# Moving the list of clipped edges and the search for leftovers from the window attention to the normalisation and the graph router's loop

## What is computed

```python
h = tok(x)                                   # patches times W
h = h + window_attention(layernorm(h))       # windows of 64 nodes, 8 heads
h = h + graph_moe(layernorm(h))              # router by attention over 262144 edges, 4 experts
h = h + image_attention(layernorm(h))        # batch norm behind it
h = h + moe(layernorm(h))                    # 8 experts, two chosen
```

```python
h = (x_flat @ W_gat).reshape(M, HEADS, NUM_EXPERTS)
e = leaky_relu(a_src[src] + a_dst[dst]);  ee = exp(e - e_max[dst])
denom = segment_sum(ee, dst);  msg = h[src] * (ee / denom[dst])
agg = segment_sum(msg, dst) + b_gat
```

## Time and profile before

| | |
|---|---|
| three runs | 872.81 us median (872.68 to 873.22) |
| the profiled execution | 871.04 us, span 869.2 us |
| busy in the span | PE 575.1, DVE 579.1, ACT 267.6, POOL 319.0 us |
| window attention | about 70 to 320 us |
| normalisation ln1 | about 320 to 348 us |
| router ahead of its loop | about 348 to 386 us |
| router's loop | about 386 to 572 us |
| mean granted TensorE clock | 0.673 of 2.4 GHz |

### The profile page before, as it was taken

The page is one execution under the profiler, slowest core; times in us unless marked ns, Lnnn a source line. Parts: engine busy times, 40 slices in busy tenths (PEclk is TensorE's granted clock), DMA queues, the critical chain, the costliest instruction groups (busy, mean ns, idle before and its releaser), DMA issues. The chain is left out here.

```text
span 869.2 us, 12176 instructions
## 1 busy us (share of the span) xinstructions
PE 575.1 (66%) x4215; PEld 346.1 (40%) x4215; DVE 579.1 (67%) x1309; ACT 267.6 (31%) x485; POOL 319.0 (37%) x373
## 2 busy tenths in 40 slices
PE   5517669756788859306766377624957772798886
PEld 4414446434466538203322233214935541522222
DVE  6985999999996472389876496566342438555453
ACT  1124223212222333013333042321043434545453
POOL 6013223122333402477777777700021110234334
PEclk9996655556688855556655565555557985589898
DMA  6100000000000000501111112000000000000001
GB/s 181 28 1 1 1 2 1 0 1 1 1 2 2 1 2 0 79 10 35 36 35 21 22 35 36 8 0 1 1 0 1 2 1 0 1 1 0 13 14 24
DMA packets 28633, 13.05 MB, mean 15 GB/s; under 512 B 22080, under 2 KB 25761, under 8 KB 28322
## 3 DMA queue, kind: packets, MB, share of 16 engines
q1 hardware_dynamic: 23842, 10.82, 5.2%
q0 software_dynamic: 4736, 1.51, 2.1%
HBM read 10.77 MB, written 1.54 MB: 14 GB/s over the span
## 5 line engine op out<-in xcount | busy, mean ns | idle before, releaser
L1453 POOL DMA_INDIRECT edge_scratch<-src_rows_dram,slot_src_index x144 | 156.7, 1088 | 46.7 <-issue 43.1
L599 POOL TENSOR_TENSOR wa_scores<-wa_scores,wa_max 128x512 f32<-128x512 f32 x32 | 37.1, 1160 | 163.5 <-DVE wa_max L780 163.5
L490 POOL TENSOR_TENSOR ln_xs<-xn,ln_stats 128x256 f32<-128x256 f32 x32 | 19.4, 615 | 154.8 <-DVE ln_stats L458 93.2
L644 PE MATMUL wa_s_ps<-wa_kbd,wa_qk 64*64 64x512 f32 x128 | 55.7, 960 | 29.8 <-issue 29.7
L543 PE MATMUL ln_pT<-ident,ln_xs 128*64 128x128 f32 (+1 forms) x112 | 28.0, 413 | 49.4 <-POOL ln_xs L490 48.7
L2054 POOL TENSOR_TENSOR moe_acc<-moe_acc,moe_weighted 128x512 f32<-128x512 f32 x28 | 37.7, 1347 | 49.7 <-DVE moe_weighted L1995 49.6
L1995 DVE SCALAR_TENSOR_TENSOR moe_weighted<-moe_y_ps,moe_b_cols,moe_G 128x512 f32<-128x512 f32 x32 | 24.0, 750 | 47.3 <-ACT moe_G L1968 43.9
L1574 PE MATMUL moe_h_ps<-xT,moe_w 65*128 65x512 f32 x64 | 54.1, 994 | 0.0
L737 ACT ACTIVATE wa_probsT<-wa_t_ps 128x512 f32<-128x512 f32 x32 | 19.1, 597 | 105.4 <-PE wa_t_ps L652 105.4
L1954 ACT ACTIVATE moe_hidden<-moe_h_ps,moe_b_cols 128x1024 f32<-128x1024 f32 x32 | 35.5, 1113 | 41.3 <-PE moe_h_ps L1886 41.3
L1894 PE MATMUL moe_y_ps<-moe_hidden,moe_w 128*64 128x512 f32 x128 | 39.0, 689 | 4.4 <-ACT moe_hidden L1954 2.3
(11 more groups left out here) (390 smaller groups left out, 1378.4 us busy)
## 6 DMA issues: line engine op xcount, KB each, us to landing
edge_onehot_T<-slot_lo_dram SPq DMA_DIRECT2D x16, 288.0 KB, 3.3
edge_scratch<-src_rows_dram,slot_src_index POOLq DMA_INDIRECT x144, 2.4
edge_scratch<-in_L_ffn_edge_index SPq DMA_DIRECT2D x2, 1024.0 KB, 6.3
xrow<-in_x SPq DMA_DIRECT2D x4, 256.0 KB, 7.8
out_h<-h SPq DMA_DIRECT2D x4, 256.0 KB, 2.6
moe_w<-in_L_ffn_W SPq DMA_DIRECT2D x3, 256.0 KB
src_rows_dram<-src_rows SPq DMA_DIRECT2D x1, 320.0 KB
moe_w<-in_L_ffn_W SPq DMA_DIRECT2D x2, 128.0 KB
```

Of the source, the lines that this page charges most:

```text
L599: pool.tensor_tensor(sc[b][:], sc[b][:], bc(mx[b][:], WIN), ALU.subtract).then_inc(shifted, 1)
L644: ins = pe.matmul(s_ps[b][half], qk[b][half, 0, :], kbd[b][half])
L1453: pool.indirect_dma_start(gs[b][:, j, :], None, srow_dram, bass.IndirectOffsetOnAxis(edges.src_index[:, x:x + 1], axis=0))\
```

## The change

The computation is the same; the order, two buffers and one engine differ.

- `PREFIX_STEP` goes from 9 to 7 and `MOVE_STEP` from 15 to 12; `take_last` is gone from the waiting loops.
- The rest of the generator waits for `now = TILES`, which only `ln1` sets. `ln1` pulls the digits of the first 512 columns and seven passes. The router's chunks pull two pieces each: four passes over 512 columns and seven over 1024, the two counts of leftovers, the digits of the last 160 columns.
- The counts of a chunk follow a table: 2, 1, 1, 1, 1, 1, 2, 3, 0, 1, 3, 3, 3, 2, 2, 2.
- `find_more` moves from ahead of the loop into chunk `REDUCE` = 8, GpSimd's reduction behind the gathers of chunk 8; the loop over the leftovers moves to chunk 9 (GpSimd: after the gathers of chunk 10).
- ScalarE does `save`, behind its GELUs.
- The router's buffers `xspread`, `hs`, `val`, `left` and `parts` move out of the memory that the leftovers lie in, into `list_onehots`.

```diff
-PREFIX_STEP, MOVE_STEP, MOVES, RING = 9, 15, 2, 6
+PREFIX_STEP, MOVE_STEP, MOVES, RING = 7, 12, 2, 6
...
-        while self.now < PREFIX_STEP + 2:
-            take_last()
+        while self.now < PREFIX_STEP + 1:
             yield
...
             while self.now <= MOVE_STEP + (j - RING) // MOVES:
-                take_last()
                 yield
...
         while self.now < TURN_STEP:
-            take_last()
             yield
...
-        while took < len(takes):
-            take_last()
+        while self.now < TILES:
             yield
-        self.after(dve, dve.memset(self.last_found[:, 512 + 8 * took:LC], 0.0))
+        self.split(dve, slice(0, 512), self.digits)
+        yield
+        took = 512
+        for start, width, passes in LAST_TAKES:
+            for _ in range(passes):
+                self.largest(dve, self.last_found[:, took:took + 8], rest[:, EC + start:EC + start + width])
+                took += 8
+                yield
+        self.after(dve, dve.memset(self.last_found[:, took:LC], 0.0))
...
-        node, digit = self.digits
-        self.after(dve, dve.tensor_scalar(node, self.last_found[:], 1.0 / M, -1.0, ALU.mult, ALU.add))
+        self.split(dve, slice(512, LC), self.late_digits)
+        yield
+
+    def split(self, dve, part, digits):
+
+
+        node, digit = (x[:, 0:part.stop - part.start] for x in digits)
+        self.after(dve, dve.tensor_scalar(node, self.last_found[:, part], 1.0 / M, -1.0, ALU.mult, ALU.add))
         self.after(dve, dve.tensor_scalar(digit, node, 6, None, ALU.arith_shift_right))
...
-    room = edges.rest[:, GX * TILES * NV:]
+    room = edges.room[:].bitcast(F32)[:, 2 * SIDE * P:]
...
-    MIDDLE = RCHUNKS // 2
+    REDUCE, MIDDLE = RCHUNKS // 2, RCHUNKS // 2 + 1
+    ends = list(itertools.accumulate((2, 1, 1, 1, 1, 1, 2, 3, 0, 1, 3, 3, 3, 2, 2, 2)))
+    assert ends[-1] == COUNT_CHUNKS
+    counts_of = [range(a, b) for a, b in zip([0] + ends, ends)]
...
-            for _ in lists:
-                pass
             match(0)
             match(1)
             spread(0)
-            edges.find_more(dve)
-            trips = dve.value_load(edges.limits[0:1, 1:2], min_val=1, max_val=XC // GX)
...
-                for u in (2 * c, 2 * c + 1):
-                    if u < COUNT_CHUNKS:
-                        count(u)
-                if c > 0:
-                    save(c - 1)
+                for _ in range(2):
+                    next(lists, None)
+                for u in counts_of[c]:
+                    count(u)
+                if c == REDUCE:
+                    edges.find_more(dve)
+                    trips = dve.value_load(edges.limits[0:1, 1:2], min_val=1, max_val=XC // GX)
...
-            gather(0)
-            edges.reduce_counts(pool)
-            for c in range(1, RCHUNKS):
+            for c in range(RCHUNKS):
                 gather(c)
+                if c == REDUCE:
+                    edges.reduce_counts(pool)
...
+            def save(c):
+
+                act.wait_ge(y_done, c + 1)
+                act.activation(ys[c % 2][c // 8][:, c // 2 % 4 * 512:(c // 2 % 4 + 1) * 512], y_ps[c % 2][:],
+                               ACT.Identity, bias=k.b2_0[:, c % 2:c % 2 + 1]).then_inc(y_saved, 1)
...
                 for u in (2 * c, 2 * c + 1):
                     gelu(u)
+                if c > 0:
+                    save(c - 1)
...
+            def pull(dve, c):
+                edges.now = TILES
+                next(lists, None)
+
             norm("ln0")
             with stage() as m:
                 window_attention(nc, m, k, xT, h, edges, lists)
-            norm("ln1", weight=k.wgat[:], out=hg, beside=lambda dve, c: next(lists, None))
+            norm("ln1", weight=k.wgat[:], out=hg, beside=pull)
```

More of the change, by code:

```diff
@@ L17 @@
+import itertools
 import math
@@ L836, in __init__ @@
         self.digits = [self.scratch[:, x * LC:x * LC + LC].bitcast(I32) for x in range(2)]
+        self.late_digits = [self.room[:].bitcast(F32)[:, 8192 + x * RC:8192 + x * RC + RC].bitcast(I32) for x in range(2)]
         self.last_lo, self.last_hi = mem.sb("last_dst_lo", [P, LC], BF16), mem.sb("last_dst_hi", [P, LC], BF16)
@@ L988, in form @@
         assert self.now < PREFIX_STEP, self.now
-        takes = [(start, width) for start, width, passes in LAST_TAKES for _ in range(passes)]
-        took = 0
-        def take_last():
-            nonlocal took
-            if took < len(takes):
-                start, width = takes[took]
-                x = 512 + 8 * took
-                self.largest(dve, self.last_found[:, x:x + 8], rest[:, EC + start:EC + start + width])
-                took += 1
-        while self.now < PREFIX_STEP + 2:
-            take_last()
+        while self.now < PREFIX_STEP + 1:
             yield
@@ L1232, in graph_router @@
     xohi = room[:, GX * P:GX * (P + TILES)].rearrange("p (c q) -> p c q", c=GX)
-    xspread = edges.rest[:, 0:GX * TILES * NV].rearrange("p (c t v) -> p c t v", c=GX, t=TILES)
     iota16 = loop.sb("iota_bf16", [P, P], BF16)
@@ L1369, in more @@
                 dve.wait_ge(more_used, i + 1)
-            def save(c):
-                dve.wait_ge(y_done, c + 1)
-                dve.tensor_scalar(ys[c % 2][c // 8][:, c // 2 % 4 * 512:(c // 2 % 4 + 1) * 512], y_ps[c % 2][:],
-                                  k.b2_0[:, c % 2:c % 2 + 1], None, ALU.add).then_inc(y_saved, 1)
             dve.memset(nobody[:, 0:W], 0.0).then_inc(nobody_ready, 1)
@@ L1442, in _ @@
             take(RCHUNKS - 1)
-            save(RCHUNKS - 1)
+            for _ in lists:
+                raise AssertionError
         @block.gpsimd
@@ L1529, in _ @@
                         act.activation(xval[:, :, :, GE], xe[:, 0], ACT.Exp).then_inc(more_exp, 1)
+            save(RCHUNKS - 1)
         @block.tensor
```

13 lines of the change are left out of this document (6 added, 7 removed).

## The result

| | before | after |
|---|---|---|
| median of four runs | 872.74 us (868.62 to 873.22) | **847.65 us** (844.64 to 852.13) |
| ratio | | 0.9746, 95% interval 0.9702 to 0.9791 |
| the profiled execution | 871.04 us, span 869.2 | 844.70 us, span 842.9 |
| mean granted TensorE clock | 0.673 | 0.706 |

The forecast was 866.9 us, range 856 to 873. The direction was right, the time 19 us too high and outside the range.

A forecast was written before the change was run, and what follows sets the result against it. The attention was taken as bound by VectorE, the router's loop by GpSimd's gathers; -13.1 + 1.5 + 3.5 - 1.4 + 3.6 = -5.9 from 871.04 gives 865.1, and 1.77 for the median makes 866.9 us, range 856 to 873.

The forecast's parts named there:

- Up to turn 22 VectorE never stands still, and the turns are as long as their edge work.: Attention: VectorE is the bound; a pass removed from turns 6 to 22 saves its length, down to an empty step's.
- Turns 6 and 7 become empty, clock at 0.50: 2 x 6.36.: Attention: these two turns, without edge work, take 6.36 us each with TensorE at 1.2 GHz, together 12.7 us.
- Turns 25 to 29 are five empty ones. I take 6.36: 31.8.: Attention: five turns without edge work take 6.36 us each, TensorE at the lower clock, together 31.8 us.
- Rival 1: Attention, turns 6, 7 and from 25: TensorE granted 2.4 GHz; total 855, or 858.4 with the last five alone; chance 0.20.
- The prelude at nothing: Router ahead of its loop: removing 17.7 us of VectorE work gains nothing, since VectorE then waits for chunk 0's rows.
- The wait at the leftovers, +3.5: Router's loop: GpSimd, having issued chunks 9 and 10, waits for the leftovers' keys from VectorE, costing 3.5 us.
- The end of the loop, +3.6: Router, chunk 15: two counts now stand before the last output, costing 3.6 us.
- rival 2: Router's loop: VectorE comes late to chunk 8, each microsecond lengthening GpSimd's wait by one; 5 give 872; chance 0.12.
- I take 0.7: Router's loop: each count beside the gathers costs GpSimd 0.7 us, so two counts moved into chunk 15 give -1.4.
- Rival 4: Router's loop: the new pieces hold up gathers as the one-hots do, costing 12 us; total 879; chance 0.08.
- The last stage at nothing: From the save of the first logits to the end, code the change doesn't touch: forecast difference 0.
- Rival 3: Attention, turns 10 to 12: the moves' matmuls come on top of a step, losing some 6 us; 873; chance 0.10.

The follow-up runs named there:

- the second chip: The changed kernel, unaltered, run again in five rounds on another chip: median 853.1 us against 868.1 for the kernel before, ratio 0.9807.

## Why the prediction was wrong, step by step

- **"Up to turn 22 VectorE never stands still, and the turns are as long as their edge work."** Right for the terms built on it: turns 8 to 19 took 100.77 (forecast 100.8), 20 to 22 took 13.97 (14.0). A pass taken out of turns 6 to 10 was worth far less than its length (26.5 us of passes gave 3.5); the forecast allowed for that with the length of an empty turn as the floor, and it is these floors that were mis-sized:
- **"Turns 6 and 7 become empty, clock at 0.50: 2 x 6.36."** Mis-sized by 2.9 us (9.78). The first empty turn took 4.48 or 4.47 in eight of ten profiles, at a clock of 0.50. VectorE waited 2.42 us in it for the reciprocal, but not for the scores as well, which stood ready, so it was no full step. In the two others (3.36 and 3.54) it was shorter still. The second took 4.1 to 6.35.
- **"Turns 25 to 29 are five empty ones. I take 6.36: 31.8."** Mis-sized by 6.4 us in the profile (25.37 at 0.81), by 3 to 6 over ten profiles (25.4 to 29.0). The forecast took one level of the clock for all of them, though the earlier trace rows showed both. Rival 1 was this mechanism. It had 1.00 in these five turns, worth 8.45 us; the clock was 0.81, and 6.4 came in this profile, 5.0 on average. Turns 23 and 24 took back 1.6.
- **The normalisation, +1.5**: +1.7. **The prelude at nothing**: right, chunk 0's wait took its place.
- **The wait at the leftovers, +3.5**: 4.09, where 0.30 stood before. **The end of the loop, +3.6**: +3.0. The chain from the search in chunk 8 over the keys to GpSimd was right in each link; VectorE did wait 2.02 us in chunk 8, so rival 2 didn't come.
- **"I take 0.7" for a count**, and with it -1.4 for the two out of the stream. This is the step that failed in the router. The price was treated as a constant that only the number of counts changes. It was 0.61 before and 0.42 after, because a gather pays only for what is left of a one-hot when it starts. So the gathers became 6.4 us cheaper and not 1.4, 5.0 more than forecast. That VectorE now reaches its counts at other moments gave this by chance; no step of the forecast had it. Rival 4, passes that hold up the gathers, is out: no gather that starts beside a pass takes over 0.95 us.
- **The last stage at nothing.** Over all profiles it can't be told from nothing (122.8 to 126.5 us in four of the kernel before and its variants, mean 125.0; 118.2 to 126.0 in twelve with the change, mean 122.8), but 8.3 of the 26.3 us between the two first profiles lie there. The forecast compared itself to one execution and gave no range to a stage of 126 us whose clock was 0.82. Nor does its 0.2% for what a measurement can tell hold: the four runs of the changed kernel spread over 7.5 us.
- Rival 3 (moves bound by TensorE) had a shadow only: 0.25 us of wait in turn 12.

The size of the change itself is then about -19 (170.8 against a mean of 189.7) + 1.7 + 1.2 (227.4 against 226.2) = -16 us, near the 15.0 measured on the second chip. The forecast missed that by 10 us, six in the attention and four to five in the gathers. The 25 us between the first chip's medians then hold some 9 more that stand in no stage's change; the profiles put 8.3 of them in the last stage.

## What to carry to other kernels

A piece of work is worth its length only where its engine is the bound *at the clock that the other engine has there*: 26.5 us of passes were worth 3.5 beside a TensorE at 1.2 GHz, and 7.5 us of them 7.4 three turns later. Where two levels of a clock appear in one stage, give each empty step both prices and let the range hold both, for every stage of the kernel, touched or not. A price paid between two free-running engines is a matter of phase, of which operation has started when the other starts: take it as a range, not as a product of count and unit price.
